# The causal mask of the row maxima, added by VectorE in its reduction instead of by a matmul

## The chip, the cores and the metric

The kernel runs on one core of one Trainium2 chip. The metric is the device time of one execution in microseconds (us), smaller is better. TensorE is PE in the profile (PEld are its weight loads), VectorE is DVE, ScalarE is ACT, GpSimd is POOL, and SyncE, which issues the DMAs, is SP.

## The reference

One transformer block on x of shape (4, 2048, 512), 16 heads of 32. LN is a layer norm without weights.

```
att = (q @ k.T) / sqrt(32), for each of the 16 heads, q, k, v from LN(x)
att = -inf where key > query, or key % 4 == 3
y   = softmax(att) @ v ;  y @ Wp + bp
x   = x + LN(that)
x   = x + LN(LN(x) @ W[idx] + b[idx])      # idx: argmax of 8 logits with noise
```

A quarter of the keys is never seen, so the kernel keeps 3 of 4 keys: 384 for each 512 tokens.

## The kernel before

The work is cut into 16 units `u`: 4 sequences by 4 blocks `j` of 512 queries. Each unit has 4 groups `g` of 4 heads `a`. For a group the kernel first finds, for every query and head, the maximum of its scores over all keys that it may see; that is the softmax's shift. Steps named "peak" do this: for each of 4 row blocks `r` of 128 queries and each head, the 384 j + 96 (r + 1) keys are cut by `chunks` into pieces of at most 512 columns, 2112 pieces in the whole kernel. TensorE writes a piece of scores into one of the two banks of `psM` (line 1004). The last piece of each row block, 1024 of the 2112, ends in the 96 keys where the causal edge runs; there TensorE adds a second matmul (line 1007), identity `IDB` by mask `MASKM`, which accumulates -1e38 onto the hidden scores. The mask is the same for every last piece. VectorE then takes the maximum of the piece (line 807) into `MP`. The last pieces have 96 to 512 columns, 278 in the mean by `chunks`.

When all peaks of a group are in, "peaks" joins them on VectorE (lines 813 to 820), "shift" turns them on TensorE (line 1014), ScalarE copies them into `MROW` (line 692), and SP sends them by two DMAs into rows 96 and 97 of `QST` (line 533), so that the score matmuls (line 1028) come out already shifted. The score blocks at the diagonal get their own mask matmul (line 1031), ScalarE takes the exponential (line 710), and TensorE forms the product with V (line 1045) and the sums (line 1061). Projections, the layer norms' statistics and the turning of tiles (lines 981 to 986, 773 to 793, 952) of neighbouring units are mixed in between.

Each engine runs a fixed list of steps in order. The lists come from the class `Order`, which plays the kernel through with a cost for every step, a rank for every step, and limited turns for shared tiles (`TURNS`: two banks of `psM`, for instance), and writes down the order in which steps start. A changed cost can so change the order of any engine's steps. TensorE may write a bank of `psM` only when VectorE has signalled `v_m` for the piece two before.

Of the kernel before, what the change touches and what calls it, by code (L numbers as in the profile page):

```python
# [9 lines left out]
def chunks(w):  # L10
    out, at = [], 0
    while w - at > 512:
        n = min(512, w - at - 96)
        out.append((at, n))
        at += n
    out.append((at, w - at))
    return out
# [30 lines left out]
class Order:  # L48
# [5 lines left out]


    LAG = {"pe": 120, "act": 180, "dve": 120, "gp": 100, "sp": 2600}
    TURNS = {"psW": 2, "open": 1, "psM": 2, "psS": 2, "SC2": 1, "QKH": 2, "XP": 2, "XTF": 2, "MHL": 2, "MROW": 2,
             "XR": 3, "SC": 1}

    def __init__(self, NB, NJ):  # L60
# [11 lines left out]
    def add(self, engine, rank, ns, name, needs=(), takes=()):  # L72
        self.steps[engine, *name] = (rank, ns, needs, takes)
# [76 lines left out]
    def attend(self, u):  # L150
        add, j = self.add, u % self.NJ
        last = 3 * j + 2
        for g in range(4):
            s = 4 * u + g
            jobs = [(r, a, ci, n) for r in range(4) for a in range(4)
                    for ci, (_, n) in enumerate(chunks(384 * j + 96 * (r + 1)))]
            for i, (r, a, ci, n) in enumerate(jobs):
                at = s - 1 + 0.85 * i / len(jobs)
                end = (r, a, ci) == (r, a, len(chunks(384 * j + 96 * (r + 1))) - 1)
                add("pe", at, n / 2.4 + 85 * end, ("peak", u, g, r, a, ci),  # L160
                    [("sp", "spread", (w, u, g)) for w in "qk"], [("psM", ("dve", "peak", u, g, r, a, ci))])
                add("dve", at, 75 + n, ("peak", u, g, r, a, ci), [("pe", "peak", u, g, r, a, ci)])
            add("dve", s - 0.2, 600, ("peaks", u, g), [("dve", "peak", u, g, r, a, ci) for r, a, ci, _ in jobs],
                [("MHL", ("pe", "shift", u, g))])
            add("pe", s - 0.2, 300, ("shift", u, g), [("dve", "peaks", u, g)], [("psM", ("act", "shift", u, g))])
            add("act", s - 0.2, 480, ("shift", u, g), [("pe", "shift", u, g)], [("MROW", ("sp", "shift", u, g))])
            add("sp", s - 0.2, 1300, ("shift", u, g), [("act", "shift", u, g)]
                + [("pe", "score", u - 1, g, 3 * ((u - 1) % self.NJ) + 2, a) for a in range(4) if u])
            free = [("act", "out", *divmod(s - 1, 4))] if s else []
            for sb in range(last + 1):  # L170
                at = s + sb / (last + 1)
                w = (512, 512, 344, 176)[max(sb - 3 * j + 1, 0)]
                exps = [("act", "exp", u, g, sb, a) for a in range(4)]
                for a in range(4):
                    add("pe", at, w / 2.4 + (85 if sb >= 3 * j else 0), ("score", u, g, sb, a),
                        [("sp", "shift", u, g), ("sp", "kcopy")],
                        [("psS", ("act", "exp", u, g, sb, a))])
                    was = self.P_WAS.get((u, g, sb))
                    held = [("dve", "wlow", 2)]
                    if was:  # L180
                        held = [("pe", "pv", *was), self.last_use(*was, a)]
                    add("act", at, 0.98 * w + 70, ("exp", u, g, sb, a), [("pe", "score", u, g, sb, a)] + held)
                add("pe", at + 0.01, 1.75 * w + 60, ("pv", u, g, sb),
                    exps + ([("pe", "pv", u, g, sb - 1)] if sb else free) + [("act", "evac", ("v", u, a)) for a in range(3)])
            before = free
# [13 lines left out]
            for i in range(4):  # L199
                add("dve", s + 1.1 + 0.02 * i, 850, ("invert", u, g, i), [("act", "out", u, g)])  # L200
            add("gp", s + 1.1, 1225, ("scale", u, g), [("dve", "invert", u, g, i) for i in range(4)])
            add("act", s + 1.1, 540, ("ohigh", u, g), [("gp", "scale", u, g)]
                + [("pe", "proj", ("p", u - 1, r), 3) for r in range(4) if u])
            add("gp", s + 1.1, 1112, ("olow", u, g), [("act", "ohigh", u, g)])
# [90 lines left out]
def sandwich_block(nc, x, Wq, bq, Wk, bk, Wv, bv, Wp, bp, Wf, bf, logits, uni, cf, cb, out):  # L295
    F32 = mybir.dt.float32
    F16 = mybir.dt.float16
    BF16 = mybir.dt.bfloat16
    I32 = mybir.dt.int32
    U32 = mybir.dt.uint32  # L300
    ALU = mybir.AluOpType
    ACT = mybir.ActivationFunctionType
# [7 lines left out]
    MW = 176  # L310
# [6 lines left out]
    with ctx:  # L317
        def sb(name, shape, dt):
            return ctx.enter_context(nc.sbuf_tensor(name, shape, dt))
# [4 lines left out]
        QST = sb("QST", [128, H, 512], F16)  # L324
# [16 lines left out]
        RC = sb("RC", [128, 2], F32)  # L341
        IDF = V[:, 13, 0:128]
        IDH = sb("IDH", [128, 128], F16)
        CB = sb("CB", [128, 128 + 96 + 3 * MW], BF16)
        ONES = sb("ONES", [128, 32], F32)
        MP = sb("MP", [128, NJ, 4, 4, 4], F32)
        MX = sb("MX", [128, 2, 4, 4], F32)
        MHL = sb("MHL", [128, 2, 4, 2, 4], F16)
        MROW = sb("MROW", [8, 2, 512], F16)
        STA = sb("STA", [128, 4, 4, 6], F32)  # L350
        MV = sb("MV", [128, 4, 4, 2], F32)
        RR = sb("RR", [128, 4, 3, 4], F32)
# [13 lines left out]
        g8 = lambda k: G8[0:1, k, :]  # L366

        IDB = CB[:, 0:128]
        MASKM = CB[:, 128:224]
        MASKT = [CB[:, 224 + MW * i:224 + MW * (i + 1)] for i in range(3)]  # L370
        stage = [P[:, 0, :, :], P[:, 1, :, :], P[:, 2, :, :], V[:, 3:7, :], V[:, 7:11, :]]
        BVB = V[:, 13, :].rearrange("p (k n) -> p k n", k=4)
        ROUND = V[0:65, 14, 0:256].bitcast(BF16)
# [98 lines left out]
        def _(e):  # L472
# [6 lines left out]
            for s in order.sp:  # L479
                kind = s[0]  # L480
                if kind == "load_x":
                    u, r = s[1:]
# [41 lines left out]
                            e.dma_start(QST[p0:p0 + 32, 4 * mt:4 * mt + 4, :], src[:, i, :]).then_inc(d_qk["q"][mt], 16)  # L524
                elif kind == "shift":
                    u, g = s[1:]
                    i = (4 * u + g) % 2
                    sp.wait_ge(a_m, AC[s])
                    sp.wait_ge(v_c, READY)
                    if u:  # L530
                        sp.wait_ge(p_qk, scored(u - 1, g))
                    for l in range(2):
                        e.dma_start(QST[96 + l:97 + l, 4 * g:4 * g + 4, :], MROW[4 * l:4 * l + 4, i, :]).then_inc(d_m[g], 16)
                elif kind == "load_r":
                    u, r = s[1:]
                    n = 4 * u + r
# [67 lines left out]
        def _(e):  # L604
            ac = Lean(e)
            for s in order.act:
# [79 lines left out]
                elif kind == "shift":  # L686
                    u, g = s[1:]
                    n = 4 * u + g
                    ac.wait_ge(p_m, PE[s])
                    if n > 1:  # L690
                        ac.wait_ge(d_m[(n - 2) % 4], 32 * ((n - 2) // 4 + 1))
                    e.activation(MROW[:, n % 2, :], psM[0:8, m_slot[s] % 2, 0:256].bitcast(F16), ACT.Copy).then_inc(a_m, 1)
                elif kind == "exp":
                    u, g, sb_, a = s[1:]
                    j, step = u % NJ, ("score", *s[1:])
# [33 lines left out]
        def _(e):  # L729
# [5 lines left out]
            for s in order.dve:  # L735
# [66 lines left out]
                elif kind == "peak":  # L802
                    u, g, r, a, ci = s[1:]
                    j = u % NJ
                    c0, n = chunks(384 * j + 96 * (r + 1))[ci]
                    dv.wait_ge(p_m, PE[s])
                    e.tensor_reduce(MP[:, j, r, a, ci:ci + 1], psM[:, m_slot[s] % 2, 0:n], AX.X, ALU.max).then_inc(v_m, 1)  # L807
                elif kind == "peaks":
                    u, g = s[1:]
# [118 lines left out]
        def _(e):  # L928
            pe = Lean(e)
            for s in order.pe:  # L930
# [64 lines left out]
                elif kind == "peak":  # L995
                    u, g, r, a, ci = s[1:]
                    j, h, k = u % NJ, 4 * g + a, m_slot[s] % 2
                    cs = chunks(384 * j + 96 * (r + 1))
                    c0, n = cs[ci]
                    last = ci == len(cs) - 1  # L1000
                    pe.wait_ge(d_qk["q"][g], 48 * (u + 1))
                    pe.wait_ge(d_qk["k"][g], 48 * (u + 1))
                    pe.wait_ge(d_cb, 16)
                    i = e.matmul(psM[:, k, 0:n], QST[0:96, h, 128 * r:128 * r + 128], KST[0:96, h, c0:c0 + n],  # L1004
                                 start=True, stop=not last)
                    if last:
                        i = e.matmul(psM[:, k, n - 96:n], IDB, MASKM, start=False, stop=True)  # L1007
                    i.then_inc(p_m, 1)
                elif kind == "shift":
                    u, g = s[1:]  # L1010
# [6 lines left out]
                elif kind == "score":  # L1017
# [8 lines left out]
                    if s_slot[s] > 1:  # L1026
                        pe.wait_ge(a_e, AC["exp", *s_job[s_slot[s] - 2][1:]])
                    i = e.matmul(psS[:, k, t0:512], KST[0:98, h, 128 * sb_:128 * sb_ + 128], QST[0:98, h, t0:512],  # L1028
                                 start=True, stop=dg < 0)
                    if dg >= 0:  # L1030
                        i = e.matmul(psS[:, k, t0:t0 + MW], IDB, MASKT[dg], start=False, stop=True)  # L1031
                    i.then_inc(p_qk, 1)
                elif kind == "pv":
# [69 lines left out]
```

## Time and profile before

| | us |
|---|---|
| runs: lowest, median, highest of 3 | 2772.9, 2775.3, 2775.33 |
| the profiled execution | 2770.63 |
| its span, first to last instruction | 2768.8 |

The span is 1.8 us shorter than the execution's own time. TensorE's mean granted clock over the span is 0.983. Busy times of the engines are shares of the span and overlap each other; a matmul's busy time holds the length of its pipeline, so back-to-back matmuls overlap in the records.

### The profile page before, as it was taken

Reading aid. Unit: us, or ns where it says so; the run is one execution under the profiler, and the core shown is the slowest. Engines: PE = TensorE matmul, PEld = TensorE weight load, DVE = VectorE, ACT = ScalarE, POOL = GpSimd, SP = SyncE. Lnnn points to the kernel's source line nnn. Section 1 sums busy time; section 2 is a strip of 40 time slices with the busy share of each in tenths; the row PEclk is TensorE's granted clock in tenths of the full one; section 3 lists DMA queues with packets and bytes.
Section 4 is the critical chain, followed back from the end, with each engine's and each line's share of the span. In section 5 each row is a group of like instructions: output and inputs, shape, how many; then the busy total and the mean of one; then the engine's idle time right before and its main releaser. Section 6 shows DMA issues by size and latency. Waiting matters only on the chain.

```text
span 2768.8 us, 46168 instructions
## 1 busy us (share of the span) xinstructions
PE 2555.6 (92%) x17416; PEld 1014.9 (37%) x17416; DVE 1972.0 (71%) x4199; ACT 1615.7 (58%) x2781; POOL 1484.0 (54%) x1350
## 2 busy tenths in 40 slices
PE   1999999999999999999999999999999999999985
PEld 0444333333343433333344433333334343333222
DVE  8667876876587687787566778678647767677623
ACT  4556656666655566566665555666665565655662
POOL 2335465665546366376653547467455635546563
PEclk7999999999999999999999999999999999999997
DMA  4211110010021111001011211101002110100000
GB/s 130 76 33 55 36 46 21 22 41 16 25 64 54 39 37 48 15 26 40 11 50 48 63 37 45 33 14 41 11 21 68 50 33 25 51 16 18 20 1 19
DMA packets 89192, 103.98 MB, mean 38 GB/s; under 512 B 11562, under 2 KB 61578, under 8 KB 88970
## 3 DMA queue, kind: packets, MB, share of 16 engines
q1 hardware_dynamic: 88970, 101.04, 12.3%
q8 instruction: 137, 2.24, 0.3%
q14 instruction: 85, 0.70, 0.1%
HBM read 39.59 MB, written 16.78 MB: 20 GB/s over the span
## 4 chain that ended last, share of the span: by engine, by line
PE 64%; DVE 22%; ACT 5%; POOL 4%; issue 3%; DMA 1%; SPq 1%; POOLq 0%; ACTq 0%; DVEq 0%
PE psO L1045 13%; PE psM L1004 11%; PE psS L1028 10%; DVE MP L807 9%; PE psU L1061 8%; PE psW L981 7%; PE psW L982 6%; PE psW L983 6%; ACT P L710 3%; DVE SC L826 2%; DVE STA L773 2%; DVE XR L785 2%; PE psS L1031 1%; DVE XP L793 1%; PE psM L1007 1%
## 5 line engine op out<-in xcount | busy, mean ns | idle before, releaser
L710 ACT ACTIVATE P<-psS,EX 128x512 f32<-128x512 f32 (+2 forms) x1920 | 1122.0, 631 | 668.3 <-PE psS L1028 357.4
L807 DVE TENSOR_REDUCE MP<-psM 128x1 f32<-128x512 f32 (+8 forms) x2112 | 1107.8, 560 | 502.1 <-PE psM L1004 269.0
L581 POOL TENSOR_TENSOR P<-P 128x512 f32<-128x512 f32 x576 | 725.5, 1288 | 119.6 <-ACT P L710 118.9
L1004 PE MATMUL psM<-KST,QST 96*128 96x512 f16 (+8 forms) x2112 | 640.0, 335 | 59.1 <-DVE MP L807 47.2
L1028 PE MATMUL psS<-QST,KST 98*128 98x512 f16 (+2 forms) x1920 | 618.9, 357 | 29.5 <-ACT P L710 22.3
L1045 PE MATMUL psO<-P,V 128*32 128x512 f32 (+2 forms) x3840 | 463.2, 554 | 10.6 <-ACT P L710 8.9
L586 POOL TENSOR_TENSOR SC<-SC 128x512 f32<-128x512 f32 x64 | 83.7, 1307 | 554.9 <-DVE SC L826 554.9
L1004 PEld LDWEIGHTS psM<-KST,QST 96*128 96x128 f16 x2112 | 200.8, 97 | 466.6 <-DVE MP L807 272.4
L1028 PEld LDWEIGHTS psS<-QST,KST 98*128 98x128 f16 x1920 | 171.1, 97 | 405.2 <-issue 190.0
L1061 PE MATMUL psU<-P,ONES 128*32 128x512 f32 (+2 forms) x2688 | 299.3, 517 | 0.0
L826 DVE RECIPROCAL SC<-SC 128x128 f32<-128x128 f32 x256 | 231.7, 929 | 79.5 <-ACT SC L718 79.5
L561 POOL TENSOR_TENSOR RR<-RR,NHALF 128x1 f32<-128x1 f32 x256 | 158.1, 623 | 210.3 <-DVE RR L778 197.7
L572 POOL TENSOR_TENSOR QKL<-SC,QKH 128x512 f16<-128x512 f32 (+1 forms) x128 | 133.8, 1046 | 198.6 <-DVE QKH L801 198.6
L1007 PE MATMUL psM<-CB 128*128 128x96 bf16 x1024 | 207.9, 207 | 0.0
L981 PE MATMUL psW<-XT,WH 128*128 128x512 f16 (+1 forms) x512 | 181.3, 354 | 4.4 <-ACT XT L652 4.4
L983 PE MATMUL psW<-XT,WH 128*128 128x512 f16 (+1 forms) x512 | 181.0, 353 | 0.0
L982 PE MATMUL psW<-XT,WL 128*128 128x512 f16 (+1 forms) x512 | 180.6, 353 | 0.0
L1031 PE MATMUL psS<-CB 128*128 128x176 bf16 x768 | 178.0, 240 | 0.0
L1045 PEld LDWEIGHTS psO<-P,V 128*32 128x32 f32 x3840 | 76.1, 108 | 165.2 <-ACT P L710 128.0
L952 PE MATMUL psW<-IDH,XP 128*128 128x128 f16 x1024 | 79.7, 222 | 52.1 <-POOL XP L567 27.7
L1061 PEld LDWEIGHTS psU<-P,ONES 128*32 128x32 f32 x2688 | 78.7, 110 | 130.9 <-issue 127.3
L773 DVE BATCH_NORM_STATS2 STA<-YX 128x6 f32<-128x512 f32 x128 | 87.4, 683 | 52.9 <-ACT YX L682 47.4
(129 smaller groups left out, 3152.7 us busy)
## 6 DMA issues: line engine op xcount, KB each, us to landing
XB<-in_L_attn_x_dram SPq DMA_DIRECT2D x64, 256.0 KB, 2.7
XR<-in_L_attn_x_dram SPq DMA_DIRECT2D x64, 256.0 KB, 2.7
QST<-QKH SPq DMA_DIRECT2D x128, 128.0 KB, 3.2
out_dram<-XR SPq DMA_DIRECT2D x64, 256.0 KB, 2.0
KST<-QKH SPq DMA_DIRECT2D x128, 96.0 KB, 2.6
QST<-QKL SPq DMA_DIRECT2D x64, 128.0 KB, 3.3
KST<-QKL SPq DMA_DIRECT2D x64, 96.0 KB, 2.7
QST<-MROW SPq DMA_DIRECT2D x128, 4.0 KB
```

What stands on the lines that cost most here:

```text
L581: e.tensor_tensor(P[:, acc, a, :], P[:, acc, a, :], P[:, buf, a, :], ALU.add).then_inc(g_s, 1)
L710: e.activation(P[:, p_buf[u, g, sb_], a, t0:512], psS[:, s_slot[step] % 2, t0:512], ACT.Exp, scale=EX[:, 1:2]).then_inc(a_e, 1)
L807: e.tensor_reduce(MP[:, j, r, a, ci:ci + 1], psM[:, m_slot[s] % 2, 0:n], AX.X, ALU.max).then_inc(v_m, 1)
L826: e.reciprocal(SC[:, 0, c], SC[:, 0, c]).then_inc(v_o, 1)
L981: e.matmul(o, lh, rh, start=kt == 0, stop=False)
L982: e.matmul(o, ll, rh, start=False, stop=False)
L983: i = e.matmul(o, lh, rl, start=False, stop=kt == 3 and bias is None)
L1004: i = e.matmul(psM[:, k, 0:n], QST[0:96, h, 128 * r:128 * r + 128], KST[0:96, h, c0:c0 + n], start=True, stop=not last)
L1007: i = e.matmul(psM[:, k, n - 96:n], IDB, MASKM, start=False, stop=True)
L1028: i = e.matmul(psS[:, k, t0:512], KST[0:98, h, 128 * sb_:128 * sb_ + 128], QST[0:98, h, t0:512], start=True, stop=dg < 0)
L1045: i = e.matmul(psO[32 * a:32 * a + 32, t0:512], V[:, vb, 32 * h:32 * h + 32], P[:, p_buf[u, g, sb_], a, t0:512], start=first, stop=last)
L1061: i = e.matmul(psU[32 * a:32 * a + 32, t0:512], ONES[:, :], P[:, buf, a, t0:512], start=sb_ == blocks[0], stop=sb_ == blocks[-1])
```

## The change

The second matmul of the last pieces is removed. VectorE takes the maximum of a last piece by `tensor_tensor_reduce`: in one call it adds the mask, widened to 512 columns (zeros in front of the 96), to the piece in `psM`, writes the sum back into the same bank, and gives the maximum to `MP`. Pieces that are not last keep `tensor_reduce`. The mask tile `CB` grows by 416 bf16 columns; `MROW` has one buffer instead of two, and ScalarE waits for the DMAs of the group before instead of those two groups before. In `Order` a last piece costs TensorE 85 ns less and VectorE 40 ns more, and `MROW` has one turn.

```diff
@@ Order: turns, and the planner's costs in attend()
-    TURNS = {"psW": 2, "open": 1, "psM": 2, "psS": 2, "SC2": 1, "QKH": 2, "XP": 2, "XTF": 2, "MHL": 2, "MROW": 2,
+    TURNS = {"psW": 2, "open": 1, "psM": 2, "psS": 2, "SC2": 1, "QKH": 2, "XP": 2, "XTF": 2, "MHL": 2, "MROW": 1,
-                add("pe", at, n / 2.4 + 85 * end, ("peak", u, g, r, a, ci),
+                add("pe", at, n / 2.4, ("peak", u, g, r, a, ci),
-                add("dve", at, 75 + n, ("peak", u, g, r, a, ci), [("pe", "peak", u, g, r, a, ci)])
+                add("dve", at, 75 + n + 40 * end, ("peak", u, g, r, a, ci), [("pe", "peak", u, g, r, a, ci)])
@@ tiles
-        CB = sb("CB", [128, 128 + 96 + 3 * MW], BF16)
+        CB = sb("CB", [128, 128 + 512 + 3 * MW], BF16)
-        MROW = sb("MROW", [8, 2, 512], F16)
+        MROW = sb("MROW", [8, 512], F16)
-        MASKM = CB[:, 128:224]
+        MASKM = CB[:, 128:640]
@@ ScalarE, shift
-                    if n > 1:
-                        ac.wait_ge(d_m[(n - 2) % 4], 32 * ((n - 2) // 4 + 1))
+                    if n:
+                        ac.wait_ge(d_m[(n - 1) % 4], 32 * ((n - 1) // 4 + 1))
@@ VectorE, peak
                     dv.wait_ge(p_m, PE[s])
+                    if ci == len(chunks(384 * j + 96 * (r + 1))) - 1:
+                        dv.wait_ge(d_cb, 16)
+                        ps = psM[:, m_slot[s] % 2, 0:n]
+                        e.tensor_tensor_reduce(out=ps, in0=ps, in1=MASKM[:, 512 - n:512], scale=1.0, scalar=-3.0e38,
+                                               op0=ALU.add, op1=ALU.max, accum_out=MP[:, j, r, a, ci:ci + 1]
+                                               ).then_inc(v_m, 1)
+                        continue
                     e.tensor_reduce(MP[:, j, r, a, ci:ci + 1], psM[:, m_slot[s] % 2, 0:n], AX.X, ALU.max).then_inc(v_m, 1)
@@ TensorE, peak
-                    pe.wait_ge(d_cb, 16)
                     i = e.matmul(psM[:, k, 0:n], QST[0:96, h, 128 * r:128 * r + 128], KST[0:96, h, c0:c0 + n],
-                                 start=True, stop=not last)
-                    if last:
-                        i = e.matmul(psM[:, k, n - 96:n], IDB, MASKM, start=False, stop=True)
+                                 start=True, stop=True)
                     i.then_inc(p_m, 1)
@@ TensorE, score
                     if dg >= 0:
+                        pe.wait_ge(d_cb, 16)
                         i = e.matmul(psS[:, k, t0:t0 + MW], IDB, MASKT[dg], start=False, stop=True)
```

The host's array for `CB` grows likewise: its mask stands in the last 96 of the 512 columns, and the 416 columns before it are zero.

## Rows read from the trace of the kernel before

**Rows 1.** Page of the profile: engines' busy times, the chain that ended last

```profile
span 2768.8 us, 46168 instructions
...
PE 2555.6 (92%) x17416; PEld 1014.9 (37%) x17416; DVE 1972.0 (71%) x4199; ACT 1615.7 (58%) x2781; POOL 1484.0 (54%) x1350
...
PE 64%; DVE 22%; ACT 5%; POOL 4%; issue 3%; DMA 1%; SPq 1%; POOLq 0%; ACTq 0%; DVEq 0%
PE psO L1045 13%; PE psM L1004 11%; PE psS L1028 10%; DVE MP L807 9%; PE psU L1061 8%; PE psW L981 7%; PE psW L982 6%; PE psW L983 6%; ACT P L710 3%; DVE SC L826 2%; DVE STA L773 2%; DVE XR L785 2%; PE psS L1031 1%; DVE XP L793 1%; PE psM L1007 1%
```

**Rows 2.** Page of the profile: costliest groups, busy and mean ns, idle before

```profile
L807 DVE TENSOR_REDUCE MP<-psM 128x1 f32<-128x512 f32 (+8 forms) x2112 | 1107.8, 560 | 502.1 <-PE psM L1004 269.0
...
L1007 PE MATMUL psM<-CB 128*128 128x96 bf16 x1024 | 207.9, 207 | 0.0
```

**Rows 3.** Timeline of PE, 1506.4 to 1507.2: start us, us, instruction

```profile
1506.72 0.23 PE L1004 MATMUL psM<-KST,QST 96*128 96x160 f16 x1
1506.79 0.21 PE L1007 MATMUL psM<-CB 128*128 128x96 bf16 x1
1506.84 0.38 PE L981 MATMUL psW<-WH,OTH 128*128 128x512 f16 x1
```

**Rows 4.** Timeline of DVE, 1646.2 to 1649.4

```profile
1645.55 0.69 DVE L773 BATCH_NORM_STATS2 STA<-XR 128x6 f32<-128x512 f32 x1 [0.16 <-ACT XR L685]
1646.28 0.18 DVE L775 BATCH_NORM_AGGREGATE MV<-STA 128x2 f32<-128x6 f32 x1
1646.50 0.15 DVE L777 TENSOR_SCALAR RR<-MV 128x1 f32<-128x1 f32 x1
1646.57 0.14 DVE L778 TENSOR_SCALAR RR<-MV 128x1 f32<-128x1 f32 x1
1646.63 1.21 DVE L807 TENSOR_REDUCE MP<-psM 128x1 f32<-128x448 f32 x2
```

**Rows 5.** Waits: engine line, waited for, us in total, times, longest us

```profile
PEld psM L1004 <- DVE MP L807: 272.4, 610, 2.2
DVE MP L807 <- PE psM L1004: 269.0, 301, 4.0
DVE MP L807 <- PE psM L1007: 223.1, 243, 2.9
...
PE psM L1004 <- DVE MP L807: 47.2, 109, 1.9
```

**Rows 6.** DVE groups by shape, 40 to 56

```profile
L893 DVE SCALAR_TENSOR_TENSOR WL<-V,SW,WH 128x2048 f16<-128x2048 f32 x2 | 5.5, 2797 | 0.0
...
L893 DVE SCALAR_TENSOR_TENSOR WL<-P,SW,WH 128x2048 f16<-128x2048 f32 x1 | 2.3, 2339 | 0.0
...
L905 DVE TENSOR_TENSOR V<-V,psW 128x512 f32<-128x512 f32 x1 | 0.7, 672 | 0.0
```

**Rows 7.** ACT groups by shape, 0 to 30

```profile
L614 ACT ACTIVATION_READ_ACCUMULATOR XR<-XR 1x1 f32 x1 | 0.2, 185 | 0.0
```

**Rows 8.** DVE lines 807 and 785 in the groups by shape, whole span

```profile
L807 DVE TENSOR_REDUCE MP<-psM 128x1 f32<-128x512 f32 x1024 | 677.4, 682 | 272.5 <-PE psM L1004 246.6 <-PE psM L1007 20.5
...
L807 DVE TENSOR_REDUCE MP<-psM 128x1 f32<-128x96 f32 x192 | 45.6, 248 | 43.1 <-PE psM L1007 42.4
```

**Rows 9.** DVE line 785, by tile: duration ns min/median/max

```profile
L785 DVE TENSOR_SCALAR XB<-XB,RR x64: 448/546/1570, 20.7 to 2220.2; 128x512 f32<-128x512 f32 x64
```

**Rows 10.** DMA issues by line: KB each, median us to landing

```profile
V<-in_L_attn_Wp_dram SPq DMA_DIRECT2D x1, 1024.0 KB, 13.1
...
CB<-in_cb_dram SPq DMA_DIRECT2D x1, 188.0 KB, 4.3
```

**Rows 11.** Timeline of SP and ACT around two row copies, 690 to 712

```profile
692.47 1.33 SPq L533 DMA_DIRECT2D QST<-MROW  x2
...
707.75 0.57 ACT L692 ACTIVATE MROW<-psM 8x512 f16<-8x512 f16 x1
```

More of the change, by code:

```diff
@@ L368, in sandwich_block @@
         IDB = CB[:, 0:128]
-        MASKM = CB[:, 128:224]
-        MASKT = [CB[:, 224 + MW * i:224 + MW * (i + 1)] for i in range(3)]
+        MASKM = CB[:, 128:640]
+        MASKT = [CB[:, 640 + MW * i:640 + MW * (i + 1)] for i in range(3)]
         stage = [P[:, 0, :, :], P[:, 1, :, :], P[:, 2, :, :], V[:, 3:7, :], V[:, 7:11, :]]
@@ L526, in _ @@
                     u, g = s[1:]
-                    i = (4 * u + g) % 2
                     sp.wait_ge(a_m, AC[s])
@@ L532, in _ @@
                     for l in range(2):
-                        e.dma_start(QST[96 + l:97 + l, 4 * g:4 * g + 4, :], MROW[4 * l:4 * l + 4, i, :]).then_inc(d_m[g], 16)
+                        e.dma_start(QST[96 + l:97 + l, 4 * g:4 * g + 4, :], MROW[4 * l:4 * l + 4, :]).then_inc(d_m[g], 16)
                 elif kind == "load_r":
@@ L689, in _ @@
                     ac.wait_ge(p_m, PE[s])
-                    if n > 1:
-                        ac.wait_ge(d_m[(n - 2) % 4], 32 * ((n - 2) // 4 + 1))
-                    e.activation(MROW[:, n % 2, :], psM[0:8, m_slot[s] % 2, 0:256].bitcast(F16), ACT.Copy).then_inc(a_m, 1)
+                    if n:
+                        ac.wait_ge(d_m[(n - 1) % 4], 32 * ((n - 1) // 4 + 1))
+                    e.activation(MROW[:, :], psM[0:8, m_slot[s] % 2, 0:256].bitcast(F16), ACT.Copy).then_inc(a_m, 1)
                 elif kind == "exp":
@@ L997, in _ @@
                     j, h, k = u % NJ, 4 * g + a, m_slot[s] % 2
-                    cs = chunks(384 * j + 96 * (r + 1))
-                    c0, n = cs[ci]
-                    last = ci == len(cs) - 1
+                    c0, n = chunks(384 * j + 96 * (r + 1))[ci]
                     pe.wait_ge(d_qk["q"][g], 48 * (u + 1))
                     pe.wait_ge(d_qk["k"][g], 48 * (u + 1))
-                    pe.wait_ge(d_cb, 16)
                     i = e.matmul(psM[:, k, 0:n], QST[0:96, h, 128 * r:128 * r + 128], KST[0:96, h, c0:c0 + n],
-                                 start=True, stop=not last)
-                    if last:
-                        i = e.matmul(psM[:, k, n - 96:n], IDB, MASKM, start=False, stop=True)
+                                 start=True, stop=True)
                     i.then_inc(p_m, 1)
@@ L1087 @@
     BIG = -1.0e38
-    cb = _np.zeros((128, 128 + 96 + 3 * 176), _np.float32)
+    cb = _np.zeros((128, 128 + 512 + 3 * 176), _np.float32)
     cb[:, 0:128] = _np.eye(128)
@@ L1091 @@
     tok = 4 * (key // 3) + key % 3
-    cb[:, 128:224] = _np.where(tok[None, 0:96] > _np.arange(128)[:, None], BIG, 0.0)
+    cb[:, 544:640] = _np.where(tok[None, 0:96] > _np.arange(128)[:, None], BIG, 0.0)
     for i, t0 in enumerate((0, 168, 336)):
-        cb[:, 224 + 176 * i:224 + 176 * (i + 1)] = _np.where(
+        cb[:, 640 + 176 * i:640 + 176 * (i + 1)] = _np.where(
             tok[128 * i:128 * i + 128, None] > t0 + _np.arange(176)[None, :], BIG, 0.0)
```

## The prediction

> **What bounds the kernel now.** I read the page's busy times first, then its chain, then the timelines of PE and DVE to learn what an instruction really takes, and last the waits. PE is busy 92% of the span, no other engine over 71%, and the chain that ended last lies on PE for 64% and on DVE for 22% [rows 1]. So PE is the main bound and DVE the second. The busy share overstates PE. A mask matmul is recorded with 207 ns [rows 2], but in the timeline the next matmul starts 0.04 to 0.05 us after it (1506.79, 1506.84), and its 160-column neighbour is followed after 0.07 [rows 3]. What counts is this distance between starts, the slot. DVE has an overlap too, a smaller one: of two statistics instructions that wait for nothing the second starts 0.07 us after the first, and the reduction behind them 0.06 us later, although each is recorded with 0.14 to 0.15 [rows 4]. One that does wait for the result of the one before it starts after the other's end: 1645.55 and 0.69 end at 1646.24, the aggregate starts at 1646.28 [rows 4].
>
> Around the change, PE and DVE hand the two banks of psM to and fro, and both wait. DVE waits 269 us for pieces without a mask and 223 us for those with one; the weight load in front of a piece waits 272 us for DVE, 610 times, most of it while PE is still working off other matmuls, since PE itself stood idle for this only 47 us [rows 5]. Neither side of the exchange is late all the time. So time taken from PE pays only in part, and so does time laid on DVE cost only in part.
>
> **Term 1, the mask matmul goes.** 1024 slots of 46 ns (between the 0.04 and 0.05 of [rows 3]; in proportion to columns, 96 of 160 of a 0.07 slot gives 42) are 47 us of PE. The page puts the mask matmul at 1% of the chain [rows 1], and 1% of 2769 us is 28 us, that is 60% of 47, near PE's own 64%. The page rounds, so 14 to 42 us. I take 28 us as gain. Its weight load goes with it and overlaps anyway: the slot holds it.
>
> **Term 2, the reduction of a last piece gets dearer.** Before, it is a reduction that reads PSUM, 682 ns at 512 columns [rows 8]. No row shows the new instruction. The part that streams is nearest to the one tensor_tensor with an input in PSUM and one in SBUF: 672 ns at 512 columns [rows 6], 10 less than the reduction, so no more per column and nothing for the second input. What comes on top is handing out the running maximum, which the program names as a separate output beside the sum. ScalarE shows such a read as an instruction of its own, 185 ns [rows 7]; a DVE instruction of one column takes a slot of 60 to 70 ns [rows 4]. Bounds per last piece: below, the 60 ns slot less 10, so 50; above, the 185 ns, plus a stream that is slower: the two groups of line 893 stand 2797 against 2339 ns for 2048 columns [rows 6], 0.22 ns a column, 62 ns at the mean of 278 columns, in all 247. Writing the sum into PSUM has no row at all; I keep it within the same upper end. I take 80 ns, near the one-column DVE slot, because the engine is the same, with 20 for the write.
>
> The Trainium skill speaks against the change here: "VectorE: DVE Perf Modes", the section on two Vector instructions with no wait between them, says that an operation that also writes out its accumulator is two instructions. No DVE row here shows one, the ScalarE row agrees in kind. With that page's fixed cost of 58 cycles at 0.96 GHz the read would be 60 ns, an estimate, and the sum below would come out about 5 us better than with my 80.
>
> How much of it counts: line 807 has 9% of the chain, 249 us, of 1107.8 us busy [rows 1, 2], so 22%. Of 1024 last pieces that is as good as 230 on the path. 230 x 80 ns = 18 us (50 gives 12, 247 gives 57). The rest hides under PE's other work. In the whole DVE's load grows by 82 us, from 71% to 74%, which leaves room.
>
> **Smaller parts.** CB grows by 416 columns of 2 bytes on 128 partitions, 104 KB. It stands ahead of the weights in SP's list. The fourth weight lands 13.1 us after its issue with 4 x 1024 KB under way [rows 10], about 310 KB per us, so 0.3 us; at CB's own 188 KB in 4.3 us it would be 2.4. I take 0.4. MROW with one buffer: in a close pair SP issues the two copies from 692.47 to 693.80 and ScalarE fills MROW again at 707.75 [rows 11], 14 us later, while a 188 KB transfer lands in 4.3 us and these have 4 KB. Nothing queues behind that wait on ScalarE: 0. If SP held the copy back longer than those 14 us, the exponentials behind the wait would stand still. The wait for d_cb moves to steps that run long after the load: 0.
>
> **Sum.** -28 + 18 + 0.4 = -9.6 us on the profiled execution, 2770.6 to 2761.0. The median of the runs is 4.7 us above that execution, so 2775.3 becomes 2765.7, say 2766, 0.35% faster. What a measurement of this kernel can tell from no change is 0.2%, 5.5 us.
>
> **The rivals.**
>
> *The read waits (slower).* If the maximum can only be read out after the stream has drained, as the aggregate waits for the statistics, the next slot opens not 0.08 us before the recorded end but 0.04 after it: 120 ns more, 180 in all, up to the 247. Then 230 x 180 to 247 ns = 41 to 57 us against 28: 2789 to 2805. The point from which it decides is 28 / 230 = 122 ns per last piece. For it: every dependent DVE pair shows that 0.04. Against: the chip may hold the maximum without a drain. "VectorE: DVE Perf Modes" in the Trainium skill, in its section on the DRAIN, says the next operation does not start until the pipe is empty; by [rows 4] independent ones start before the recorded end.
>
> *A port shared with GpSimd (slower, far).* Line 785 on DVE takes 546 ns in the median and up to 1570 [rows 9], while POOL is busy for 54% of the span [rows 1]. The new instruction reads its mask from SBUF, the old one nothing. If it suffered the mean of such delays, here 242 ns (its mean of 788 [rows 8] against 546), 230 x 322 ns = 74 us against 28: 2821. Against: the mask is a single SBUF input. By the Trainium skill, "SBUF — State Buffer", section "Who interferes with whom", an instruction with at most one SBUF input outside the two-port modes does not contend with GpSimd; nothing in this trace tests it.
>
> *Gain hidden.* PE arrives earlier at a bank that DVE gives back later. If only 14 us of the 28 come through, the sum is +4: 2780.
>
> *The order.* The planner charges PE 85 ns less and DVE 40 more per last piece, so all lists can come out otherwise. Its 85 ns were 39 above the slot of 46, so the new costs of PE fit the trace better. PE's 47 us of idleness before pieces [rows 5] are what a better mix could win; half is 24, and that gives 2742. A worse mix by the same amount gives 2790.
>
> **How the numbers follow.** Forecast 0.36, with its own range from 2759 (50 ns) to 2775 (120 ns): 0.27 of it faster, 0.09 within. The read waits 0.22. Port 0.05. Hidden 0.12, within 0.2%. Order better 0.15, worse 0.10. Faster 0.27 + 0.15 = 0.42; same 0.09 + 0.12 = 0.21; slower 0.22 + 0.05 + 0.10 = 0.37. The range from 2745 to 2800 leaves out the port, half of the better order, the far end of the waiting read and a tail of the worse order, together about 0.2.
>
> **What the profile after would show.** The mask matmul's 1024 rows on PE are gone, and PE's busy time is lower by up to 208 us. On DVE the last pieces stand as a group of 1024, with a second group of the same number if the read is an instruction; what the next start is behind it gives term 2, with 50 to 120 ns for the forecast and 180 or more for the waiting read. Wide scatter of the new instruction where POOL is busy would show the port. DVE's chain share rises from 22% by about 1%, PE's falls by about 1%. Waits of ScalarE on MROW's copies would show the single buffer. I am wrong if the slot grows by more than 122 ns or the order of steps decides more than both terms.

## The result, and the profile after

Four executions of the changed kernel took 2798.1 to 2799.5 us, median 2799.15; four of the kernel before, beside them on the same chip, 2774.73. The ratio is 1.0096 [1.0084, 1.0108]: 24 us slower by the medians, 27 by the ratio, where 10 us faster was forecast. The profiled execution has a span of 2797.2 us against 2768.8, and a mean granted clock of 0.971 against 0.983.

The page of the kernel after, in the parts that answer to [rows 1, 2] (line numbers have moved: 1004 is now 1007, the old reduction 813, the new instruction 809):

```profile
span 2797.2 us, 45135 instructions
...
PE 2551.1 (91%) x16392; PEld 964.3 (34%) x16392; DVE 2014.0 (72%) x5223; ACT 1615.0 (58%) x2781; POOL 1479.8 (53%) x1350
...
PE 60%; DVE 23%; POOL 6%; ACT 5%; issue 4%; DMA 1%; SPq 1%; POOLq 0%; ACTq 0%; DVEq 0%
...
L809 DVE DVE_READ_ACCUMULATOR2_ANT MP<- 128x1 f32 x1024 | 144.4, 141 | 0.0
```

1024 matmuls are gone from PE (17416 to 16392), yet its busy time fell by 4.5 us only, although their group was recorded with 207.9 [rows 2]: what was taken away overlapped other matmuls, and other rows of PE grew. (With the steps in their old order the same removal takes 24 us off PE's busy time: 2532.0 us in e1_old_order, below.) DVE has exactly 1024 instructions more (4199 to 5223): the reading out of the accumulator is an instruction, as "VectorE: DVE Perf Modes" of the Trainium skill states in its section on two Vector instructions with no wait between them.

Groups of DVE by shape, kernel after:

```profile
L813 DVE TENSOR_REDUCE MP<-psM 128x1 f32<-128x512 f32 x960 | 641.9, 683 | 265.7 <-PE psM L1007 261.9
...
L809 DVE CUSTOM_DVE_ANT_0 psM<-psM,CB 128x96 f32<-128x96 f32 x192 | 49.1, 263 | 53.0 <-PE psM L1007 51.6
...
L809 DVE CUSTOM_DVE_ANT_0 psM<-psM,CB 128x512 f32<-128x512 f32 x64 | 44.3, 692 | 15.2 <-PE psM L1007 15.2
```

The new instruction is 9 ns dearer than the reduction at 512 columns (692, 683) and 15 ns at 96 (263 against the 248 of [rows 8]). Timeline of DVE, kernel after; columns are start, duration, instruction:

```profile
700.41 0.30 DVE L809 CUSTOM_DVE_ANT_0 psM<-psM,CB 128x96 f32<-128x96 f32 x1
700.62 0.14 DVE L809 DVE_READ_ACCUMULATOR2_ANT MP<- 128x1 f32 x1
...
1186.22 0.38 DVE L809 CUSTOM_DVE_ANT_0 psM<-psM,CB 128x224 f32<-128x224 f32 x1
1186.53 0.14 DVE L809 DVE_READ_ACCUMULATOR2_ANT MP<- 128x1 f32 x1
1186.53 0.95 DVE L832 RECIPROCAL SC<-SC 128x128 f32<-128x128 f32 x1
1187.39 1.22 DVE L813 TENSOR_REDUCE MP<-psM 128x1 f32<-128x512 f32 x2
```

The reciprocal starts in the same moment as the read (1186.53), 0.07 us before the recorded end of the main instruction (1186.60). The trace of the kernel after shows the same elsewhere: where the next DVE instruction starts before the main one's recorded end, 589 times, it does so 83 ns before it in the median, as it does behind a plain reduction, and 499 times in the same nanosecond as the read. So the read takes no slot of DVE that could be seen. But it ends at 1186.67, and only then is the bank of psM given back: over all 1024 pieces the read ends 56 to 61 ns after the main instruction (median 58), and `v_m` is counted 10 to 11 ns after the end of a read as after that of a plain reduction. What a last piece costs is therefore 9 to 15 ns of DVE's time and 58 ns of delay in the release, about 70 ns for whoever waits for it. That is near the 80 ns that were taken; its kind is another.

Waits of the kernel after, the rows that answer to [rows 5]; columns are us in total, times, longest:

```profile
DVE MP L813 <- PE psM L1007: 284.8, 325, 3.9
...
PEld psM L1007 <- DVE MP L813: 205.9, 403, 2.0
...
DVE psM L809 <- PE psM L1007: 200.6, 191, 3.0
...
PEld psM L1007 <- DVE MP L809: 138.8, 317, 1.7
...
PE psM L1007 <- DVE MP L813: 38.2, 84, 1.7
...
PE psM L1007 <- DVE MP L809: 26.8, 60, 1.3
```

PE now stands idle for DVE's banks for 38.2 + 26.8 = 65 us in 144 waits, where it was 47 us in 109, and its weight loads 345 us against 272. These waits are not the 24 us, though. e1_old_order, which has the same instructions and loses nothing, has nearly as much:

```profile
PE psM L1007 <- DVE MP L813: 35.0, 77, 1.9
...
PE psM L1007 <- DVE MP L809: 24.7, 66, 1.0
```

ScalarE waits for nothing on account of the single MROW.

### The profile page after: what moved, and what is told of

It reads as the page before. It is cut to its first block, busy times and chain, and to the rows that moved or that the text cites. A ratio compares the mean times of both kernels' runs of the same rounds, so it can differ in the third digit from the quotient of the medians.

```text
span 2797.2 us, 45135 instructions
## 1 busy us (share of the span) xinstructions
PE 2551.1 (91%) x16392; PEld 964.3 (34%) x16392; DVE 2014.0 (72%) x5223; ACT 1615.0 (58%) x2781; POOL 1479.8 (53%) x1350
## 4 chain that ended last, share of the span: by engine, by line
PE 60%; DVE 23%; POOL 6%; ACT 5%; issue 4%; DMA 1%; SPq 1%; POOLq 0%; ACTq 0%; DVEq 0%
PE psO L1047 12%; PE psM L1007 10%; PE psS L1029 9%; PE psU L1063 7%; PE psW L987 6%; DVE MP L813 6%; PE psW L988 6%; PE psW L989 6%; ACT P L709 4%; DVE psM L809 3%; DVE SC L832 3%; DVE STA L772 2%; POOL P L580 2%; DVE XR L784 2%; PE psS L1033 1%
## 5 line engine op out<-in xcount | busy, mean ns | idle before, releaser
L813 DVE TENSOR_REDUCE MP<-psM 128x1 f32<-128x512 f32 (+1 forms) x1088 | 719.2, 677 | 289.0 <-PE psM L1007 284.8
L1007 PE MATMUL psM<-KST,QST 96*128 96x512 f16 (+8 forms) x2112 | 636.1, 340 | 78.9 <-DVE MP L813 38.2
L1029 PE MATMUL psS<-QST,KST 98*128 98x512 f16 (+2 forms) x1920 | 628.8, 361 | 33.0 <-ACT P L709 27.9
L809 DVE CUSTOM_DVE_ANT_0 psM<-psM,CB 128x96 f32<-128x96 f32 (+5 forms) x1024 | 453.3, 452 | 205.9 <-PE psM L1007 200.6
L1007 PEld LDWEIGHTS psM<-KST,QST 96*128 96x128 f16 x2112 | 194.3, 97 | 531.3 <-DVE MP L813 205.9
L809 DVE DVE_READ_ACCUMULATOR2_ANT MP<- 128x1 f32 x1024 | 144.4, 141 | 0.0
L566 POOL TENSOR_TENSOR XP<-XR,XP 128x512 f16<-128x512 f32 x64 | 75.0, 1175 | 107.3 <-DVE XP L792 107.2
```

What stands on the lines that cost most here:

```text
L809: e.tensor_tensor_reduce(out=ps, in0=ps, in1=MASKM[:, 512 - n:512], scale=1.0, scalar=-3.0e38, op0=ALU.add, op1=ALU.max, accum_out=MP[:, j ...
```

## The experiments

All runs stand beside runs of the kernel before on the same chip; the ratio is to them, with its 95% interval. Two things changed at once: the *instructions* (mask matmul out, new reduction in, MROW, CB) and three numbers of the planner `Order`, which set the *order* of steps on all engines. The lists written with one or two turns of MROW are the same step for step, so two numbers remain: what a last piece adds to PE's cost and to DVE's. I write them as a pair: before is (85, 0), after is (0, 40).

### Instructions against order

The first four kernels cross the two. The instruction theory: the reduction's price on the path exceeds the matmul's. The order theory: the two numbers of the planner decide.

**e1_old_order**, the changed kernel with the order of before:

```diff
-                add("pe", at, n / 2.4, ("peak", u, g, r, a, ci),
+                add("pe", at, n / 2.4 + 85 * end, ("peak", u, g, r, a, ci),
-                add("dve", at, 75 + n + 40 * end, ("peak", u, g, r, a, ci), [("pe", "peak", u, g, r, a, ci)])
+                add("dve", at, 75 + n, ("peak", u, g, r, a, ci), [("pe", "peak", u, g, r, a, ci)])
```

(and two turns of MROW in `TURNS`)

> All instructions of the changed kernel (mask in VectorE's reduction, single MROW buffer, wide CB), but the planner's three numbers as before, so every engine runs its steps in the order of before. Theory 'order' (the new planner costs made a worse mix): without them the change is worth what the prediction's terms say with the measured DVE slot (next start about 10 ns later instead of 80), so 2755 to 2770 us. Theory 'release' (the bank comes back about 70 ns later, behind the accumulator read, PE waits more and its granted clock drops more often): the order doesn't matter, 2790 to 2800. Theory 'clock' (PE without its mask matmuls falls to half clock more often, whatever DVE does): also 2785 to 2800, with half-clock stretches as in the changed kernel.

Measured: 2774.07 us, 0.9992 [0.9982, 1.0002]. The 24 us are gone with two numbers of the planner. The time lies 4 us above the 2755 to 2770 that the theory "order" had given, and far below what the two others gave.

**e2_new_order**, the kernel before, its instructions untouched, with the planner's numbers of after:

```diff
-                add("pe", at, n / 2.4 + 85 * end, ("peak", u, g, r, a, ci),
+                add("pe", at, n / 2.4, ("peak", u, g, r, a, ci),
-                add("dve", at, 75 + n, ("peak", u, g, r, a, ci), [("pe", "peak", u, g, r, a, ci)])
+                add("dve", at, 75 + n + 40 * end, ("peak", u, g, r, a, ci), [("pe", "peak", u, g, r, a, ci)])
```

> The kernel before with its mask matmuls and plain reductions, and only the planner's three numbers changed (last piece 85 ns less on PE, 40 more on DVE, one turn of MROW), so that its steps run in the order of the changed kernel. Theory 'order': the loss comes with it, 2795 to 2815 (the changed kernel's 2799 plus what the mask matmuls cost). Theory 'release' and theory 'clock': 2770 to 2780, no change.

Measured: 2803.17 us, 1.0096 [1.008, 1.0111]. The old instructions in the new order lose all that the changed kernel loses. The instruction theory is out; the order makes the loss, whatever the instructions.

**e3_no_mask**, the kernel before in its own order, without the mask matmul and with nothing for it. It prices term 1 alone:

```diff
                     i = e.matmul(psM[:, k, 0:n], QST[0:96, h, 128 * r:128 * r + 128], KST[0:96, h, c0:c0 + n],
-                                 start=True, stop=not last)
-                    if last:
-                        i = e.matmul(psM[:, k, n - 96:n], IDB, MASKM, start=False, stop=True)
+                                 start=True, stop=True)
```

> The kernel before, in its old order, without the mask matmuls and with nothing in their place: the row maxima are taken over hidden keys too, the rest is computed as before. It is term 1 alone. Theories 'order' and 'release': PE's 28 us on the chain come back, 2745 to 2755. Theory 'clock': the freed time turns into gaps and half clock, 2770 to 2795.

Measured: 2762.61 us, 0.9951 [0.9938, 0.9965], so 0.49% of 2775 us = 13.6 us gained, half of the 28 that the chain share had promised, and outside the ranges of all three theories. The waits of e3_no_mask show a part of the rest:

```profile
DVE MP L807 <- PE psM L1004: 481.6, 539, 3.9
PEld psM L1004 <- DVE MP L807: 300.7, 668, 2.2
...
PE psM L1004 <- DVE MP L807: 55.4, 125, 1.9
```

DVE's wait for pieces fell from 492 us (269 + 223 in [rows 5]) by 10 only, and PE waits longer for DVE: 55 us for 47, and its weight loads 301 for 272. PE comes earlier to a bank that comes back no sooner.

The granted clock takes another part. Its mean over the executions is 0.9790 here and 0.9783 in e1_old_order, both without the mask matmul in the old order; with it, it is 0.9811 (before) and 0.9807 (e4_mask_twice, next). A fall of 0.0021 is at most 6 us of full-speed time in 2775. That is what the theory "clock" said in kind; in size it is far from the 24 us.

**e4_mask_twice**, the changed kernel in the old order, with the mask matmul put back on top. Against before, it prices term 2 alone:

```diff
                     i = e.matmul(psM[:, k, 0:n], QST[0:96, h, 128 * r:128 * r + 128], KST[0:96, h, c0:c0 + n],
-                                 start=True, stop=True)
+                                 start=True, stop=not last)
+                    if last:
+                        i = e.matmul(psM[:, k, n - 96:n], IDB, MASKM[:, 416:512], start=False, stop=True)
```

> The changed kernel in the old order, with the mask matmuls kept as well, so the mask is added twice (the maxima stay the same). It is term 2 alone against the kernel before. Theory 'order': 230 pieces on the chain by 10 to 70 ns, 2777 to 2791. Theory 'release': at least 2800, above the changed kernel. Theory 'clock': 2775 to 2785, since PE keeps its mask matmuls.

Measured: 2785.98 us, 1.0033 [1.0021, 1.0045], 9 us, half of the 18. Together -13.6 + 9.2 = -4.4 us, against -2.2 measured in e1 (interval -5.0 to +0.6).

**h1_new_order_mask_twice** came in the last round, and asks whether the new order only wants its filling: it was planned as if the mask matmul were not there, and perhaps with it the loss would be another. The edit is that of e4 on the changed kernel as it is.

> The changed kernel in its own, new order, with the mask matmuls kept as well (mask added twice, maxima the same). In the old order the mask matmuls cost 11 us on top of VectorE's masking (2786 against 2774). Theory 'terms hold in any order': 2799 + 9 to 15 = 2808 to 2814. Theory 'PE needs its filling' (without the mask matmuls PE falls to half clock more often here, mean granted clock 0.971 against 0.977 with them): 2795 to 2804, with a clock near 0.977.

Measured: 2818.45 us, 1.0166 [1.0149, 1.0182]. Against the changed kernel's 1.0096 the mask matmul costs 0.70% here, 19 us (0.41%, 11 us, in the old order: 1.0033 against 0.9992), and the new reduction again 0.70% (against e2). Both terms hold in sign in either order, and are larger in the worse one. That PE lacked work to fill the new order fell: the time is above the ranges of both theories. The mean clock, 0.9738, lies between the changed kernel's 0.971 and the 0.977 of e2.

### Which number of the planner

Four kernels with the changed kernel's instructions ask which of the two numbers, and whether numbers that fit the measured slots are best (the slot of the mask matmul is gone, 0; the new reduction takes some 10 ns more of DVE). The edits are in these two lines alone, with the pair put in place of 0 and 40:

```diff
-                add("pe", at, n / 2.4, ("peak", u, g, r, a, ci),
+                add("pe", at, n / 2.4 + 85 * end, ("peak", u, g, r, a, ci),
...
-                add("dve", at, 75 + n + 40 * end, ("peak", u, g, r, a, ci), [("pe", "peak", u, g, r, a, ci)])
+                add("dve", at, 75 + n + 10 * end, ("peak", u, g, r, a, ci), [("pe", "peak", u, g, r, a, ci)])
```

**f1_pe_cost_old**, (85, 40), the first hunk alone:

> The changed kernel with TensorE's planner cost of a last piece back at 85 ns more; VectorE's stays 40 ns more. So of the two numbers that alter the order only VectorE's is new. Theory 'PE number' (the order is bad because the planner thinks PE free too early): 2770 to 2780. Theory 'DVE number': 2790 to 2805. Theory 'any order' (the old order is a fortunate one, and most others cost): 2782 to 2805.

Measured: 2763.18 us, 0.9952 [0.9936, 0.9969]. The best ratio of all kernels here that mask: faster than both kernels by one number, a cost for a matmul that is no longer there. No theory had it: the lowest range began at 2770.

**f2_dve_cost_old**, (0, 0): `75 + n` without the 40.

> The changed kernel with VectorE's planner cost of a last piece back at no surcharge; TensorE's stays without its 85 ns. Theory 'PE number': 2790 to 2805. Theory 'DVE number': 2770 to 2780. Theory 'any order': 2782 to 2805.

Measured: 2791.16 us, 1.0052 [1.0035, 1.0068]. PE's number brings most of the loss; DVE's 40 adds to it here, and helps beside PE's 85.

**f3_true_costs**, (0, 10), the second hunk alone:

> The changed kernel planned with what its trace shows: nothing on PE for the mask, 10 ns more on VectorE for a last piece (the distance between starts: 605 against 597 ns at 512 columns). If an order is bad because its costs are wrong, this one should be the best of all: below 2774. Theory 'any order': 2782 to 2805, true costs don't help.

Measured: 2782.86 us, 1.0023 [1.0014, 1.0033]. That is better than (0, 0) and (0, 40), but worse than the costs of before, and not the best of all, as was expected if true costs were what counts. Costs nearer to the chip don't by themselves give a good order.

**f4_one_ns**, (84, 0): e1 with one ns less in PE's number.

> The changed kernel planned with the costs of before, except that a last piece costs TensorE 84 ns more instead of 85. That moves 1486 of PE's 6257 steps, one of them by 291 places. Theories 'PE number' and 'DVE number': a nanosecond is nothing, 2770 to 2778, as with the old order. Theory 'any order': 2780 to 2800.

Measured: 2786.48 us, 1.0035 [1.0022, 1.0048], 0.43% above e1. So PE's number doesn't act through its size. A nanosecond tips a choice of the planner somewhere and the lists behind it are others.

### What in the order

Laying the written lists side by side, I found two late places in f4's that e1's hasn't: in units 5 and 9 steps of the last row block of a unit's output half stand further down PE's list, the turn at line 958 by 291 places and the four projection steps that follow it by 282, more than a group of heads. Steps that stand 100 places or more from where e1's list has them I call long moves. One step behind the turn is ScalarE's evacuation into XF (line 643), for the same unit and row block in e1_old_order

```profile
1052.58 1.02 ACT L643 ACTIVATE XF<-psW 128x1024 f16<-128x1024 f16 x1 [1.40 <-PE psW L958]
```

and in f4_one_ns

```profile
1178.76 1.02 ACT L643 ACTIVATE XF<-psW 128x1024 f16<-128x1024 f16 x1 [0.32 <-PE psW L958]
```

126 us later. The changed kernel's order has moves of 130 to 412 places for units 6, 7, 9 and 12. One more step, in unit 8, stands 105 places off. They are not all of one kind: those of units 8 and 9 stand later, by up to 291 places; those of 6, 7 and 12 stand earlier, by up to 412. The theory "long moves" says that an order with such moves costs time; "the PE number" says that a higher number is better; "any order" says that it is chance.

**g1_dve40_mask_mm**, before's instructions with (85, 40), no long moves:

```diff
-                add("dve", at, 75 + n, ("peak", u, g, r, a, ci), [("pe", "peak", u, g, r, a, ci)])
+                add("dve", at, 75 + n + 40 * end, ("peak", u, g, r, a, ci), [("pe", "peak", u, g, r, a, ci)])
```

> The kernel before, mask matmuls and plain reductions as they were, with one number of the planner changed: a last piece costs VectorE 40 ns more. Its steps run in the order of the run that was faster by 0.5%. If that gain is the order's alone: 2760 to 2768, and the instructions are worth nothing here as in the old order. If it needs the new instructions: 2773 to 2780.

Measured: 2767.8 us, 0.9969 [0.9957, 0.998]. The order of f1 gains with the old instructions too; the new instructions add 0.17% to it (0.9952 [0.9936, 0.9969]; the intervals overlap). So in three orders the change of instructions came to -0.07% (e1 against before), 0.00% (the changed kernel against e2) and -0.17%.

The others have the changed kernel's instructions, and a pair each in the lines of the hunk above. **g2_86**, (86, 0), no long moves:

> The changed kernel planned with the costs of before, except 86 ns instead of 85 for TensorE's last piece: 99 of 6257 PE steps move, none by more than 5 places. Theory 'long moves' (a loss comes where projections and turns of the second half of a unit slip by some 300 to 400 places, most of a group): no long move here, so 2770 to 2777, as the old order. Theory 'any order': 2780 to 2790, like 84 ns.

Measured: 2776.88 us, 0.9999 [0.9988, 1.001].

**g3_130_40**, (130, 40), with long moves:

> The changed kernel with 130 ns for TensorE's last piece and 40 for VectorE's. Theory 'PE number' (too cheap a PE gives the bad orders, so a dearer one gives good ones): 2755 to 2770. Theory 'long moves' (steps move by up to 412 places against the old order, the same kind of steps as in the changed kernel): 2780 to 2800.

Measured: 2779.05 us, 1.0009 [1.0, 1.0019]. A PE number of 130 is worse than 85; "the PE number" fell. "Long moves" had said 2780 to 2800, and missed by 1 us.

**g4_45_40**, (45, 40), with long moves:

> The changed kernel with 45 ns for TensorE's last piece, half way, and 40 for VectorE's. Theory 'PE number': half way between 2763 (85 ns) and 2799 (0 ns), 2775 to 2787. Theory 'long moves' (up to 410 places): 2785 to 2800. Theory 'any order', without a rule: anything from 2760 to 2805.

Measured: 2788.32 us, 1.0049 [1.0032, 1.0065], where long moves gave 2785 to 2800 and "the PE number" 2775 to 2787.

**h2_84_40**, (84, 40), no long moves:

> The changed kernel planned with 84 and 40 ns, one less for PE than the fast run (85 and 40, 2763 us): 762 PE steps move, at most 69 places. Theory 'long moves': no step leaves its part of the queue, 2758 to 2770. Theory 'no rule' (each order is a draw with about 0.4% spread): 2763 to 2790, and then most likely above 2770.

Measured: 2761.63 us, 0.9962 [0.9949, 0.9975]. The same ns that cost 0.43% beside DVE's 0 costs 0.1% or nothing beside its 40.

**h3_87_40**, (87, 40), with long moves:

> The changed kernel planned with 87 and 40 ns: against the fast run 1757 PE steps move, one group of them by 295 places, as between 85 and 84 with the old VectorE cost, which took 12 us. Theory 'long moves': 2770 to 2780. Theory 'no rule': 2763 to 2790.

Measured: 2776.68 us, 1.0013 [1.0002, 1.0024].

**h4_85_44**, (85, 44), with long moves:

> The changed kernel planned with 85 and 44 ns: against the fast run 3236 PE steps move, by up to 417 places. Theory 'long moves': 2775 to 2795. Theory 'costs near 85 and 40 are good in themselves': 2758 to 2768.

Measured: 2771.25 us, 0.9995 [0.9986, 1.0005], faster than long moves let expect.

All orders with the changed kernel's instructions, sorted by ratio; the last two columns are means over the executions:

```
order        long moves   ratio    granted clock   span, us
(85, 40)     no           0.9952   0.9825          2760.3
(84, 40)     no           0.9962   0.9827          2759.9
(85, 0)      no           0.9992   0.9783          2772.2
(85, 44)     yes          0.9995   0.9803          2769.4
(86, 0)      no           0.9999   0.9764          2774.8
(130, 40)    yes          1.0009   0.9797          2776.3
(87, 40)     yes          1.0013   0.9781          2773.0
(0, 10)      yes          1.0023   0.9762          2780.6
(84, 0)      yes          1.0035   0.9761          2784.5
(45, 40)     yes          1.0049   0.9758          2786.2
(0, 0)       yes          1.0052   0.9782          2789.6
(0, 40)      yes          1.0096   0.971           2797.2
```

No order without long moves is slower than before, and of the eight with them two can't be told from it: (85, 44), and (130, 40), whose interval begins at 1.0. Two comparisons speak for the moves. The same ten steps move between (85, 0) and (84, 0) and between (85, 40) and (87, 40), and the ratio rises by 0.43% and 0.61%. Two speak against them as the cause. (85, 44) and (45, 40) have the same 36 long moves, to within 93 places, and differ by 0.54%; (130, 40) has 21 of the 26 long moves of the changed kernel's (0, 40), all but those of unit 12, and is 0.87% faster. And between (85, 0) and (85, 40), which differ by 0.40%, no step moves by more than 75 places. Long moves go with a loss, but don't set its size, and which of the many shorter moves count stays open. The granted clock goes with the time too, with (0, 0) and (86, 0) as outliers.

### How an order costs time

The clock is seen in the kernel after in a row of three windows; the columns are the stretch and its length, busy time and instructions of PE, PEld, DVE, ACT and POOL, then the granted clock (1.00 is 2.4 GHz, 0.50 is 1.2), DMA share and GB/s:

```profile
1178.80:1185.40 6.60, 6.30 (x54) 3.29 (x53) 5.41 (x13) 3.42 (x8) 0.00 (x0) 1.00 0.00 1
1185.40:1188.80 3.40, 1.85 (x8) 0.53 (x7) 3.40 (x8) 2.80 (x6) 0.00 (x0) 1.00 0.03 6
1188.80:1199.00 10.20, 9.72 (x33) 2.00 (x36) 7.30 (x15) 4.91 (x8) 6.92 (x6) 0.50 0.25 64
```

In the middle stretch DVE is busy without a gap and PE is busy for 1.85 of 3.40 us; behind it PE works at half its clock for 10.2 us. PE's timeline in this stretch:

```profile
1185.19 0.26 PE L1007 MATMUL psM<-KST,QST 96*128 96x224 f16 x1
1186.37 0.75 PE L1007 MATMUL psM<-KST,QST 96*128 96x512 f16 x2 [0.92 <-DVE MP L813]
1186.95 0.60 PE L1029 MATMUL psS<-QST,KST 98*128 98x512 f16 x2
1188.08 0.27 PE L1007 MATMUL psM<-KST,QST 96*128 96x224 f16 x1 [0.53 <-DVE MP L813]
```

The next step in PE's list is a piece each time, and PE waits 0.92 and 0.53 us for its bank, while DVE has reciprocals of 0.95 us between its reductions (timeline above). So one such neighbourhood in the lists is paid for twice, by what this place shows: 1.45 us of idleness, and then the clock. Half-clock stretches that begin between 100 us from the start and 100 us from the end make up 92 us in the kernel after, 58 in e2_new_order, 38 in e1_old_order, 31 in the kernel before and 24 in f1.

The other part is PE's idle time. The span without its first and last 100 us, in before, e2_new_order, e1_old_order and the kernel after; columns as above, so length and PE's busy time stand first:

```profile
100.00:2668.80 2568.80, 2453.63 (x16863) 973.49 (x16860) 1872.08 (x3937) 1540.57 (x2658) 1409.30 (x1275) 0.99 0.12 36
...
100.00:2699.30 2599.30, 2470.69 (x16875) 978.20 (x16871) 1879.30 (x3939) 1541.83 (x2657) 1407.07 (x1276) 0.99 0.12 35
...
100.00:2666.50 2566.50, 2431.61 (x15868) 920.30 (x15867) 1908.71 (x4935) 1536.48 (x2657) 1406.83 (x1275) 0.99 0.12 36
...
100.00:2697.20 2597.20, 2450.90 (x15878) 924.98 (x15875) 1914.05 (x4939) 1541.83 (x2660) 1406.12 (x1276) 0.98 0.12 35
```

PE is idle for 115 us before and 129 in e2, so the new order adds 13 us with the old instructions; it is idle for 135 us in e1 and 146 in the changed kernel, so the order adds 11 with the new ones. The profiled spans differ by 30.5 and 30.7 us; the rest is PE's busy time, which holds the half-clock stretches.

How much is the clock's? From the mean of 0.9811 (sixteen executions of before) to 0.971 is 0.0101, or 28 us of full-speed time at most in 2775; the loss of span is 22 against these sixteen, which did not run beside it. In e2 the mean is 0.9768: 12 us at most, and the loss 26. So the clock can be all of it in the one and under half in the other, for the same order, and at least 14 us of e2 are no change of clock; PE's 13 us of idleness are near that. Executions of one and the same kernel give a second measure. Among the eleven of e1_old_order the longest span, 2778.9 us, has a clock of 0.975 and the shortest, 2766.5, one of 0.981: about 2 us for 0.001. By that, an estimate, the clock is some 20 of the changed kernel's 22 us and some 9 of e2's 26. No run changed the clock alone, and waits can make both numbers worse together, so its share stays open.

## Why the prediction was wrong

**The sum assumed the old order: this is the step that failed.** It put the two planner's numbers among the rivals, as "the order", with 0.10 for worse and half of PE's idleness, 24 us, as the price. The price was right (e2: 26 us), the place and the chance were not. A changed cost could change every list, as the text before the diff says, and no row of before tells which way; so the order was not a rival beside a sum of 10 us but the largest term, of unknown sign, and the sum had it at nothing. Its extent could have been read before the run, by writing out both lists of `Order`: 4945 of PE's 6257 steps stand elsewhere in the new one. The only argument given for its sign, that the new PE costs fit the measured slots better, does not hold: f1 (0.9952 with the 85) and f3 (1.0023 with costs close to the slots) stand against it.

**Term 1** had the right sign and twice the size: 28 us said, 13.6 measured (e3). The slot of 46 ns was not the fault: it is the median of the 905 mask matmuls in the trace of before that the next matmul overlaps. The chain's share was: 60% of a slot, read from the chain, is what would be saved if nothing else came last instead. Measured it was 13.6 of 47 us, 29%. Of the missing 14 us the longer waits for banks are 8 (55 against 47), and the lower clock, which the prediction had nowhere, up to 6.

**Term 2** likewise: 18 said, 9 measured (e4). The price per last piece, 80 ns, came out at 9 to 15 ns of slot and 58 ns of release, about 70. If all of that counts on the path, 230 pieces were too many by nearly half; but no run parts the slot from the release, and 1024 pieces at 9 ns of slot alone would give 9 us as well. Which factor failed stays open. As the two errors partly cancel, which is luck, the sum of the instructions, -9.6, missed e1's -2.2 by only 7 us; the lower clock of e1 (0.9783 for 0.9811) is up to 8.

**Smaller parts**: MROW at 0 and CB near 0 can't be told apart from nothing in e1.

**The rivals.** The read does not wait for a drain: the next instruction starts with it, before the recorded end. The port shared with GpSimd: the 64 instructions at 512 columns average 692 ns, and none of the 1024 takes over 700, so no scatter like that of line 785 [rows 9], with POOL busy for 53% of the span. The mean of 788 that the prediction takes from [rows 8] stands in this line of the kernel before:

```profile
L785 DVE TENSOR_SCALAR XB<-XB,RR 128x512 f32<-128x512 f32 x64 | 50.2, 788 | 7.7 <-POOL RR L561 7.6
```

The Trainium skill's rule in "SBUF — State Buffer", section "Who interferes with whom", that one SBUF input does not contend, agrees. Gain hidden: true for half of term 1, by e3's waits and its clock. The order, worse: this happened.

**The marks named beforehand.** The 1024 rows are gone and the new group of reads is there. "PE's busy time lower by up to 208 us" held at 4.5 in the changed kernel. DVE's load grew by 42 us (1972.0 to 2014.0), not 82: where the next instruction follows at once, the read lies over it. DVE's chain share rose by one point as said, PE's fell by four, not one, POOL's rose from 4% to 6%. The chain of e1_old_order, then that of e2_new_order:

```profile
PE 60%; DVE 25%; ACT 6%; POOL 4%; issue 3%; DMA 1%; SPq 1%; POOLq 0%; ACTq 0%; DVEq 0%
...
PE 64%; DVE 22%; ACT 5%; POOL 4%; issue 3%; SPq 1%; DMA 1%; POOLq 0%; ACTq 0%; DVEq 0%
```

PE's 60% came with the instructions, and the new order with the old instructions has before's shares (64, 22, 4) although it loses 26 us. Chain shares don't show what an order costs. The condition "the order of steps decides more than both terms" is the one that was met.

## What to carry to other kernels

Where a static order is computed from costs, an edit to a cost is a change of its own, of unknown sign and here ten times the size of the instructions' effect: run the old instructions in the new order and the new in the old before judging either. The planner's costs are knobs, not facts; with new instructions try a few neighbours and keep the best that was measured. A share of the chain promised about twice what the removal gave.

## What the runs showed of the hardware that was not expected

- Reading out the accumulator is an instruction of 141 ns on DVE that takes no slot that could be seen: what comes next starts in the same nanosecond in 499 of 589 cases. It delays the signal of its result by 58 ns all the same.
- An add with a running maximum, from PSUM and SBUF and back into the same bank of PSUM, streams nearly as fast as a plain reduction from PSUM: 692 against 683 ns at 512 columns. Adding, writing back and the maximum together cost 9 ns there and 15 at 96 columns.
- Executions of one and the same kernel differ in their mean granted clock, and the time goes with it: 0.981 at 2766.5 us and 0.975 at 2778.9 in e1_old_order.
- After 3.4 us in which PE was busy for 1.85, it was granted 1.2 GHz for 10.2 us, in which it was busy for 9.72.
